# Slot weights by a difference and tanh, mask constants and half of the norm's rows on ScalarE, in the opening of a one-core transformer block

## What is computed

```python
mod = (silu(c) @ wmod).reshape(4, 6, 1, 128); sa, ca, ga, sb, cb, gb = ...
h = layernorm(x) * (1 + ca) + sa
q, k, v = h @ wq, h @ wk, h @ wv            # 16, 4, 4 heads of 64
logits = h @ wr                             # 16 heads, 4 nodes
tk_vals, tk_idx = top_k(logits, 2); tk_w = softmax(tk_vals)
member = one_hot(tk_idx, 4).sum(-2) > 0; pos = cumsum(member) - member
for n in range(4):                          # rotary at pos[..., n], causal, keys of node n only
    probs = softmax(where(causal & member[..., n], qr @ kr.T * 64**-0.5, -1e9)); outs[n] = probs @ v
y = (tk_w[..., None] * take(outs, tk_idx)).sum(3)
x = x + ga * (y @ wo)
x = x + gb * moe(layernorm(x) * (1 + cb) + sb)   # 8 routed choices, one is none, and a shared expert
```

## Time and profile before

| | us |
|---|---|
| median of 3 runs | 1045.87 |
| lowest and highest | 1040.52, 1046.56 |
| the profiled execution's own time | 1042.09 |
| its span | 1040.3 |
| TensorE busy | 880.0 (85%) |
| VectorE busy | 776.9 (75%) |
| ScalarE busy | 748.7 (72%) |
| GpSimd busy | 617.7 (59%) |

### The profile page before, as it was taken

The page is one execution under the profiler, slowest core; times in us unless marked ns, Lnnn a source line. Parts: engine busy times, 40 slices in busy tenths (PEclk is TensorE's granted clock), DMA queues, the critical chain, the costliest instruction groups (busy, mean ns, idle before and its releaser), DMA issues.

```text
span 1040.3 us, 18878 instructions
## 1 busy us (share of the span) xinstructions
PE 880.0 (85%) x5651; PEld 608.0 (58%) x5651; DVE 776.9 (75%) x1840; ACT 748.7 (72%) x2024; POOL 617.7 (59%) x869
## 2 busy tenths in 40 slices
PE   4338989999998998999899989999999996867883
PEld 3326656666666666656666657666676655534552
DVE  6999969957987797789778867996776755445443
ACT  6327787888888888877987888878887885333441
POOL 3157757857886786778677866886665630240222
PEclk9669989999999999999999999999999997789996
DMA  9000001001000000010000000010000041020003
GB/s 217 5 1 7 12 16 28 23 12 33 22 22 23 22 22 22 23 32 23 20 24 22 23 22 22 26 29 8 3 3 2 3 182 61 13 86 1 19 24 97
DMA packets 45602, 32.66 MB, mean 31 GB/s; under 512 B 8032, under 2 KB 43488, under 8 KB 45504
## 3 DMA queue, kind: packets, MB, share of 16 engines
q1 hardware_dynamic: 44288, 28.95, 9.7%
q0 software_dynamic: 1216, 2.51, 0.7%
HBM read 18.30 MB, written 12.36 MB: 29 GB/s over the span
## 4 chain that ended last, share of the span: by engine, by line
PE 63%; DVE 23%; ACT 6%; issue 5%; another core or an unknown queue 1%; POOL 1%; DMA 0%; ACTq 0%; DVEq 0%; POOLq 0%; SPq 0%
PE psum L1126 21%; PE psum L1148 7%; PE psum L1233 6%; PE psum L1140 6%; PE psum L1067 5%; PE psum L1111 4%; DVE pcs L805 3%; PE psum L1131 3%; DVE arena L753 3%; ACT probs L549 3%; DVE accs L861 2%; PE psum L1169 2%; DVE psum L850 2%; PE psum L1113 2%; PE psum L1128 2%
## 5 line engine op out<-in xcount | busy, mean ns | idle before, releaser
L1126 PE MATMUL psum<-QK 128*128 128x128 f32 (+3 forms) x1024 | 372.9, 449 | 4.9 <-ACT QK L528 4.9
L549 ACT ACTIVATE probs<-psum,negmax 128x128 f32<-128x128 f32 (+3 forms) x512 | 267.3, 530 | 108.3 <-DVE negmax L850 75.1
L390 POOL TENSOR_TENSOR R<-pcs 128x512 f32<-128x512 f32 x128 | 207.2, 1639 | 64.1 <-DVE pcs L805 46.8
L850 DVE CUSTOM_DVE_ANT_0 psum<-psum,causal 128x384 f32<-128x384 f32 (+1 forms) x256 | 156.9, 636 | 75.5 <-PE psum L1131 75.3
L1126 PEld LDWEIGHTS psum<-QK 128*128 128x128 f32 x1024 | 164.8, 193 | 49.3 <-issue 41.2
L416 POOL TENSOR_TENSOR coef<-rden,wslot 128x2 f32<-128x2 f32 x256 | 68.3, 267 | 177.2 <-DVE rden L856 177.1
L805 DVE TENSOR_TENSOR pcs<-psum,arena 128x512 f32<-128x512 f32 x256 | 161.6, 672 | 0.0
L861 DVE SCALAR_TENSOR_TENSOR accs<-probs,coef,accs 128x128 f32<-128x128 f32 (+3 forms) x256 | 157.6, 616 | 1.0 <-ACT accs L558 1.0
L558 ACT ACTIVATE accs<-probs,coef 128x128 f32<-128x128 f32 (+3 forms) x256 | 148.6, 581 | 11.5 <-POOL coef L416 10.7
L1140 PE MATMUL psum<-ident,accs 128*128 128x128 f32 x640 | 116.3, 280 | 46.5 <-ACT QK L528 41.9
L528 ACT ACTIVATE QK<-psum 128x384 f32<-128x384 f32 x256 | 126.7, 495 | 0.9 <-PE psum L1113 0.7
(11 more groups left out here) (211 smaller groups left out, 1473.3 us busy)
## 6 DMA issues: line engine op xcount, KB each, us to landing
weight_halves<-whl SPq DMA_DIRECT2D x48, 128.0 KB, 2.2
arena<-weight_halves SPq DMA_DIRECT2D x7, 768.0 KB, 7.1
wst<-in_L_ffn_w_up_dram SPq DMA_DIRECT2D x14, 128.0 KB, 2.6
wst<-in_L_ffn_w_gate_dram SPq DMA_DIRECT2D x14, 128.0 KB, 2.5
wst<-in_L_ffn_w_down_dram SPq DMA_DIRECT2D x14, 128.0 KB, 2.5
sorted_rows<-arena SPq DMA_DIRECT2D x1, 1430.0 KB, 12.1
QK<-sorted_rows SPq DMA_DIRECT2D x5, 260.0 KB, 4.0
x<-in_L_attn_x_dram SPq DMA_DIRECT2D x4, 256.0 KB, 4.1
```

The source lines that it names most:

```text
L390: pool.tensor_tensor(R[u][:, :, :, 0:3:2, half * HALF:(half + 1) * HALF].rearrange("p t e j f -> p (t e) j f"), halves(pc, half), halves(p ...
L549: act.activation((expB if e else expA)[:, k % (4 if e else 3), 0:w], area, ACT.Exp, scale=1.0 if k % TB < 2 else -1.0, bias=negmax[k % 4][ ...
L850: dve.tensor_tensor_reduce(score_area(k, e), score_area(k, e), causal[:, T - w:T], -1.0, 3e38, ALU.add, ALU.min, accum_out=negmax[k % 4][: ...
L1126: pe.matmul(o, QK[:, u, e, rows], QK[:, u, 2, 0:w], start=True, stop=False)
```

## The change

- The slot weights are no softmax over four logits but one difference: the logit of slot A less that of slot B, by `sA - sB` times the logits, summed (three VectorE operations after `first_angles(0)`); ScalarE makes tanh of half of it and from it both weights, 0.5 + 0.5 tanh and 0.5 - 0.5 tanh, between `trigonometry(0, 0)` and `trigonometry(0, 1)`. Five VectorE operations (L828 to L837) and one exponential are gone. The table preloaded there is now Silu's in place of Sin's.
- `cgap`, the reciprocal of the code difference (which is -1, -2 or -3), is made by a polynomial: two operations in place of `reciprocal`.
- Mask constants: a column `big_row`, 32768 at partition 32 and zero elsewhere, is made first on GpSimd; ScalarE writes the ring from it with scale 1 and -1, two activations for each buffer in place of one. The two GpSimd writes into partition 32 are gone.
- Norm, first turn only: ScalarE normalizes the last two of every four tiles (Identity with a scale and a bias column), VectorE the other two, after one more small operation for the bias.
- The scaling of the query weights (L478) moves behind the copies of the logits on ScalarE.

```diff
 @@ gpsimd
-            for t_, v in ((zero, 0.0), (ident, 0.0), ...
+            pool.memset(zero[:, :], 0.0).then_inc(S["const_done"], 1)
+            pool.wait_ge(S["const_done"], 1)
+            pool.affine_select(out=big_row[:, :], in_=zero[:, :], compare_op=ALU.not_equal, fill=BIG, base=-32,
+                               pattern=[[-1, 1]], channel_multiplier=1).then_inc(S["big_done"], 1)
+            for t_, v in ((one_half, 0.5), (ident, 0.0), ...
...
-            pool.wait_ge(S["zeros_done"], RING + 1)
+            pool.wait_ge(S["zeros_done"], 2 * RING + 1)
...
-            pool.wait_ge(S["ident_done"], 7)
-            pool.wait_ge(S["zero_set"], 2)
-            pool.memset(mring[32:33, :, 0, :], BIG).then_inc(S["mm_init"], 2)
-            pool.memset(mring[32:33, :, 1:3, :], -BIG).then_inc(S["mm_init"], 2)
-            pool.wait_ge(S["mm_init"], 4)
...
-            pool.wait_ge(S["w_done"], 1)
+            pool.wait_ge(S["w_done"], 2)
 @@ scalar
+            def mask_rows(r):
+                for kinds, sign in ((slice(0, 1), 1.0), (slice(1, 3), -1.0)):
+                    t_ = mring[:, r, kinds, :]
+                    act.activation(t_, big_row[:, :].unsqueeze(2).to_broadcast([P, t_.shape[1], T]), ACT.Copy, scale=sign
+                                   ).then_inc(S["zeros_done"], 1)
...
-            act.wait_ge(S["wr_in"], 32)
-            act.activation(w_qk[:, :, 0, :], w_qk[:, :, 0, :], ACT.Copy, scale=HD ** -0.5).then_inc(S["wq_scaled"], 1)
...
+                if turn == 0:
+                    act.wait_ge(S["rs_step"], 5)
+                    for t_ in range(NT):
+                        if t_ % TB >= 2:
+                            act.activation(xn[:, t_, :], x1[:, t_, :], ACT.Identity, bias=rs[:, 2, t_:t_ + 1],
+                                           scale=rs[:, 1, t_:t_ + 1]).then_inc(S["xn_a"], 1)
...
-            act.preload_act_table(ACT.Sin)
+            act.wait_ge(S["wr_in"], 32)
+            act.activation(w_qk[:, :, 0, :], w_qk[:, :, 0, :], ACT.Copy, scale=HD ** -0.5).then_inc(S["wq_scaled"], 1)
+            act.preload_act_table(ACT.Silu)
...
             trigonometry(0, 0)
+            act.wait_ge(S["w_step"], 3)
+            act.activation(lmax[:, 0, :], lmax[:, 0, :], ACT.Tanh, scale=0.5).then_inc(S["w_tanh"], 1)
+            act.wait_ge(S["w_tanh"], 1)
+            for e in range(2):
+                act.activation(wslot[:, :, e], lmax[:, 0, :], ACT.Identity, scale=0.5 - e, bias=one_half[:, 0:1]
+                               ).then_inc(S["w_done"], 1)
             trigonometry(0, 1)
             act.preload_act_table(ACT.Exp)
-            act.wait_ge(S["l_sub"], 1)
-            act.activation(ew[:, :], ew[:, :], ACT.Exp).then_inc(S["l_exp"], 1)
 @@ vector, normalize(turn)
+                if turn == 0:
+                    dve.scalar_tensor_tensor(rs[:, 2, :], mv[:, :, 0], -1.0, rs[:, 1, :], ALU.mult, ALU.mult
+                                             ).then_inc(S["rs_step"], 1)
                 for t_ in range(NT):
+                    if turn == 0 and t_ % TB >= 2:
+                        continue
 @@ vector, after first_angles(0)
-            dve.tensor_reduce(lmax[:, 0, :], L, AX_X, ALU.max).then_inc(S["l_max"], 1)
-            dve.wait_ge(S["l_max"], 1)
-            dve.tensor_tensor(W, L, lmax[:, 0, :].unsqueeze(2).to_broadcast([P, NS, NODES]), ALU.subtract
-                              ).then_inc(S["l_sub"], 1)
+            dif = prod[:, :, 0, :]
+            dve.tensor_tensor(dif, sA, sB, ALU.subtract).then_inc(S["w_step"], 1)
+            dve.wait_ge(S["w_step"], 1)
+            dve.tensor_tensor(dif, dif, L, ALU.mult).then_inc(S["w_step"], 1)
+            dve.wait_ge(S["w_step"], 2)
+            dve.tensor_reduce(lmax[:, 0, :], dif, AX_X, ALU.add).then_inc(S["w_step"], 1)
...
-            dve.reciprocal(cgap[:, :], lmax[:, 1, :]).then_inc(S["codes_done"], 1)
+            dve.scalar_tensor_tensor(cgap[:, :], lmax[:, 1, :], 6.0, lmax[:, 1, :], ALU.add, ALU.mult
+                                     ).then_inc(S["gap_done"], 1)
+            dve.wait_ge(S["gap_done"], 2)
+            dve.tensor_scalar(cgap[:, :], cgap[:, :], 11.0, -1.0 / 6.0, ALU.add, ALU.mult).then_inc(S["codes_done"], 1)
             first_angles(1)
             for e in range(2):
                 products(1, e)
-            dve.wait_ge(S["l_exp"], 1)
-            dve.tensor_tensor(prod[:, :, :, :], W.unsqueeze(2).to_broadcast([P, NS, 2, NODES]), sel[:, :, :, :],
-                              ALU.mult).then_inc(S["pr_w"], 1)
...
-            dve.tensor_reduce(es[:, :, :], prod[:, :, :, :], AX_X, ALU.add).then_inc(S["w_step"], 1)
...
-            dve.tensor_tensor(lmax[:, 1, :], es[:, :, 0], es[:, :, 1], ALU.add).then_inc(S["w_step"], 1)
...
-            dve.reciprocal(lmax[:, 0, :], lmax[:, 1, :]).then_inc(S["w_step"], 1)
...
-            dve.tensor_tensor(wslot[:, :, :], es[:, :, :], lmax[:, 0, :].unsqueeze(2).to_broadcast([P, NS, 2]),
-                              ALU.mult).then_inc(S["w_done"], 1)
 @@ tensor, norm_rows(turn)
-                    pe.wait_ge(S["xn_done"], turn * NT + (b + 1) * TB)
+                    if turn:
+                        pe.wait_ge(S["xn_done"], NT // 2 + (b + 1) * TB)
+                    else:
+                        pe.wait_ge(S["xn_done"], (b + 1) * TB // 2)
+                        pe.wait_ge(S["xn_a"], (b + 1) * TB // 2)
```

More of the change, by code:

```diff
@@ L63, in block_kernel @@
         zero = sb("zero", [P, 1])
+        one_half = sb("one_half", [P, 1])
+        big_row = sb("big_row", [P, 1])
         freq = sb("freq", [P, HALF])
@@ L196, in block_kernel @@
         names = """c_in wr_in loaded x_in0 x_in1 x_in2 x_in3 out_done const_done ident_done
[L197 to L200, removed]
+            mm_in0 mm_in1 mm_in2 c_exp c_sum c_rec c_silu mod_mm mod_raw mod_sign mod_mag mod_done
+            gcol_done ga_mm ga_ev wq_scaled bn_s bn_a var_e std_dev rs_step xn_done xn_a xn_t h_ready zeros_done big_done
+            lg_mm lg_ev rank_s rank_m w_tanh l_mem mem16 sel_a sel_b sel_cp code_p code_e gap_done
+            codes_done pos_mm pr_pos slots_w mk_t mk_ev w_step w_done
             ang_mul ang_k ang_n ang_r1 ang_r2 ang_clamp ang_abs trig_done qk_mm prod_done add_done q_done kd_done
@@ L295, in _ @@
             sp.wait_ge(S["mk_ev"], 6)
-            sp.wait_ge(S["mm_init"], 4)
+            sp.wait_ge(S["zeros_done"], 2 * RING + 1)
             for n in range(NH):
@@ L335, in _ @@
         def _(pool):
-            for t_, v in ((zero, 0.0), (ident, 0.0), (ident16, 0.0), (identbig, 0.0), (causal, 0.0), (before, 1.0),
+            pool.memset(zero[:, :], 0.0).then_inc(S["const_done"], 1)
+            pool.wait_ge(S["const_done"], 1)
+            pool.affine_select(out=big_row[:, :], in_=zero[:, :], compare_op=ALU.not_equal, fill=BIG, base=-32,
+                               pattern=[[-1, 1]], channel_multiplier=1).then_inc(S["big_done"], 1)
+            for t_, v in ((one_half, 0.5), (ident, 0.0), (ident16, 0.0), (identbig, 0.0), (causal, 0.0), (before, 1.0),
                           (ones16, 1.0), (ones, 1.0), (half_pi, float(np.pi / 2))):
@@ L340, in _ @@
                       allow_small_or_imprecise_dtypes=True).then_inc(S["const_done"], 1)
-            pool.wait_ge(S["const_done"], 10)
+            pool.wait_ge(S["const_done"], 11)
             for t_, v in ((ident, 1.0), (ident16, 1.0), (identbig, BIG)):
@@ L354, in _ @@
                       allow_small_or_imprecise_dtypes=True).then_inc(S["const_done"], 1)
[L355 to L356 removed]
+            pool.wait_ge(S["const_done"], 15)
+            pool.wait_ge(S["zeros_done"], 2 * RING + 1)
             pool.iota(zero_rows[:, :, DIM + 1].bitcast(U32), [[P, SORTED]], base=TOKENS, channel_multiplier=1
@@ L462, in _ @@
         def _(act):
[L463 to L467, removed]
+            def mask_rows(r):
[3 more added lines that the diff above has]
+                                   ).then_inc(S["zeros_done"], 1)
             act.wait_ge(S["const_done"], 1)
+            act.wait_ge(S["big_done"], 1)
             for r in range(2):
-                zeros(mring[:, r, :, :])
+                mask_rows(r)
             act.wait_ge(S["c_in"], 32)
@@ L474, in _ @@
             act.preload_act_table(ACT.Sqrt)
-            zeros(mring[:, 2, :, :])
-            zeros(zero_rows[:, :, :])
-            act.wait_ge(S["wr_in"], 32)
-            act.activation(w_qk[:, :, 0, :], w_qk[:, :, 0, :], ACT.Copy, scale=HD ** -0.5).then_inc(S["wq_scaled"], 1)
+            mask_rows(2)
+            act.activation(zero_rows[:, :, :], zero[:, :].unsqueeze(2).to_broadcast([P, SORTED, ROW]), ACT.Copy
+                           ).then_inc(S["zeros_done"], 1)
             def norm(turn, which, dst):
@@ L666, in normalize @@
                 dve.reciprocal(rs[:, 0, :], sd[:, :]).then_inc(S["rs_step"], 1)
-                dve.wait_ge(S["rs_step"], 4 * turn + 1)
+                dve.wait_ge(S["rs_step"], 5 * turn + 1)
```

(11 more changed lines are left out.)

7 lines of the change are left out of this document (removed).

## The result

The changed kernel takes 1036.89 us (median of 9 runs, 1035.15 to 1038.37) against 1046.56 of before (9 runs, 1040.33 to 1047.86). The ratio is 0.9928, 95% interval 0.9906 to 0.995. The profiled execution took 1035.15 us with a span of 1033.4, which is 6.9 less than before's span. The forecast was 1037.5, or -8.3 us from the median of before's first three runs. By the ratio the change is -7.5 us (-9.8 to -5.2); the quotient of the two medians, 0.9908, gives -9.7, since before's own times spread from 1040 to 1048.

A forecast was written before the change was run, and what follows sets the result against it. The opening was taken as a serial chain, mostly through VectorE, which stays the bound for a while behind it. Terms: -3.0 + 0.4 - 5.1 - 0.6 = -8.3 us, giving 1037.5 us as median; range 1030.5 to 1043, 8 in 10.

The forecast's parts named there:

- Modulation, -3.4: Opening, VectorE's small modulation operations: without GpSimd's mask writes, about 0.65 us in place of 4.07, so -3.4 us.
- Start, +0.25: Very start: ScalarE's split mask fills cost +0.25 us; GpSimd's new column is ready under ScalarE's first table load.
- Norm on two engines: Opening's norm: earlier tiles and transposes end the logits at 21.6 instead of 24.6 us; -3.0 including start and modulation.
- The logits' duration: Router logits on TensorE, behind the norm's transposes: taken to last 3.54 us, as in the old trace.
- second rival: Whole kernel, gain larger than forecast: -11.5 us, 1034 us; chance 0.20.
- Slot weights and loop start, +0.4 - 5.1: From slot weights to first row maximum: GpSimd's start comes 0.4 us later, the first row maximum 5.1 us earlier.
- Clock, -0.6: First scores: without TensorE's 4.93 us pause, early product pairs run at full clock; -0.6 of a possible 0 to -1.4 us.
- I carry the whole of it to the end: Attention loop: its steps depend only on each other, so the whole -8.3 us reaches the kernel's end.
- more than the sum: Attention loop: all 1.4 us of clock arrives and one later TensorE pause with slow restart vanishes; 1034 us, chance 0.20.
- The slower rival: First heads: TensorE's small waits grow to pauses costing 1.4 us each; with ten, 1051.5 us; chance 0.04.
- The ends of the sum, -10.4 and -6.5: Whole kernel: the total gain in us with all terms at their best and at their worst.
- The table loads: ScalarE around tanh and sine: a switch costs at most 1.3 us; two extra loads stay hidden or make the sum -7.3.

The follow-up runs named there:

- b_mask: Kernel before with only the mask constants changed (ScalarE writes the ring from a column, GpSimd's two writes gone); ratio to before 0.9989 (0.9966 to 1.0011).
- a_best2: Changed kernel plus 12 idle matmuls before the norm's transposes, 14 before the first scores, and ScalarE's table load first, second run; ratio to before 0.988.
- a_warm1: Changed kernel plus 12 idle TensorE matmuls ahead of the norm's transposes; ratio to before 0.9909 (0.9876 to 0.9942).
- a_norm_dve: Changed kernel with all 16 tiles of the norm on VectorE again; ratio to before 0.9943 (0.9919 to 0.9966).
- b_weights: Kernel before with only the slot weights changed (difference, tanh, polynomial for the gap); ratio to before 0.9964 (0.9935 to 0.9992).
- a_again2: Changed kernel, unedited, profiled once more on another chip; one run, 1024.48 us.
- b_again: Kernel before, unedited, run again as a kernel of its own; ratio to before 1.0006 (0.9983 to 1.0028).
- b_warm1: Kernel before plus 12 idle TensorE matmuls ahead of the norm's transposes; ratio to before 0.999 (0.9968 to 1.0012).
- a_sin: Changed kernel with the table preloaded for Sin in place of Silu; one run, 1024.40 us.
- a_again: Changed kernel, unedited, run again on another chip; ratio to before 0.9931 (0.9899 to 0.9963).

## Why the prediction was right

*Modulation, -3.4.* Right. The operations take 0.70 us (11.90 to 12.60) where they took 4.16 (11.04 to 15.20), and they do so with GpSimd's writes gone and nothing else changed in the norm (b_mask).

*Start, +0.25.* Mis-sized: 0.86 (11.04 to 11.90). The step that failed is that "GpSimd's new column is ready under ScalarE's first table load". The load itself came behind the wait for the column, at 1.40 us and not 0.81; put ahead of it, it gives 0.6 back (a_best2). The rest is the split fills, as forecast.

*Norm on two engines.* The durations were right (a tile every 0.39 us; ScalarE's copies late next, seen as 0.70 us in a_warm1). But the split gives nothing, since the transposes bound the stage from 14.7 on either way: they start and end alike in a_norm_dve. Whether it would give something behind the idle matmuls was not tried. "3.70 us whatever feeds them" is itself a duration at the low clock: behind the idle matmuls they take 2.94 (a_warm1). A slip of the sum: 17.95 + 3.54 is 21.5, not 21.6. With fast logits the whole stands at 22.7 to 23.4 instead of 22.2 for the start of the ranks, -1.9 to -2.6 against -3.0.

*The logits' duration.* The step that fails is the unsaid one in "then the logits start, which took 3.54 us": a duration read from one trace at 2.4 GHz was taken as the code's. It is 4.3 or 7.1 in traces of one program, and 3.7 in others with the same logits code. In after's trace this term alone turned some -2.5 into +0.85. That the profiled span still came out near the forecast is luck: the loop gave 3.6 us that the forecast had left out (its second rival hadn't). The ratio over nine executions, where such draws mix, is nearer to a test of the sum, with 2.3 us either way.

*Slot weights and loop start, +0.4 - 5.1.* Right in sum: -5.1 in b_weights, and -4.4 to -5.2 in all kernels with the part and without the second group of idle matmuls, by how much of the first scores is slow: the stretch at 0.50 ends between 71 and 72 us in a_again2 and between 74 and 75 in after. The +0.4 was +0.25 in after (from the ranks to the second angles 30.40 us, before 30.15), since the gap's first operation was cheaper than its row (0.42 us and not 0.6). One reason given is not the one: ScalarE's exponential didn't keep it from QK. The copy that ended TensorE's pause of 4.93 us stood in ScalarE's list behind L549, which had waited 6.43 us for the late first row maximum.

*Clock, -0.6.* Right in kind, somewhat smaller. The pause of 4.93 us and its fall are gone from all ten traces with the new weights and present in before, b_again, b_mask and b_warm1 (from 76 to 80 us on). From the first row maximum to that of the second head it takes 10.41 to 10.68 us in these four and 9.98 or 9.99 in eight of the ten, so -0.4 to -0.7. In a_warm1 it takes 10.16, and in after, whose first scores were slow longest, 10.44: there the term gave nothing.

*"I carry the whole of it to the end".* Not in one execution. The loop's length follows the count of falls: 694.6 to 694.9 us with one, 695.9 to 696.5 with two, 697.2 to 698.4 with three, 699.1 and 699.6 with four, so about 1.5 us each, near the 1.4 that the prediction gave a slow restart. After's trace had two falls fewer than before's: by this price 3 of the 3.6 us that its loop was shorter, which hid that the logits had lost as much. Whether the gain arrives whole on average is not shown: the ratio allows 5.2 to 9.8 us. The rival "more than the sum" had this mechanism; it came together with a start that was smaller than forecast. The slower rival needed six falls more; no trace had more than four. The ends of the sum, -10.4 and -6.5, are wider than the bounds given for its terms, which add up to -10.0 and -7.0.

*The table loads.* The trace agrees with the 1283 ns of the Trainium skill (ScalarE: Activation LUTs, What ACT_TABLE_LOAD costs): 1.28 us in a_sin. The drain of 1380 ns that it adds doesn't show: in the earlier trace rows the exponential starts 0.01 us behind its load. With Silu's table preloaded, sine, tanh and sine ran without a load between them (after); with Sin's, tanh and the second sine had one each (a_sin), which cost nothing here.

Open: what decides whether a pause of TensorE ends in a fall. A fall between 139 and 149 us comes in 11 of the 14 traces, one between 204 and 216 in 6, in kernels with and without the change, and nothing tried here says beforehand in which. With the idle matmuls ahead of the transposes the logits took 3.76 us in three of three traces of the changed kernel; without them the length is a draw. That the new weights lower their number is not shown beyond the one at 79.

## What to carry to other kernels

Before a duration on TensorE goes into a sum, compare it with the same shape elsewhere: 421 ns against 275 for one matmul, or 7.06 us against 3.68 for the group, was the clock level here, and it may be the other one next time. A gain in an opening ahead of a loop with pauses arrives only give or take a fall or two; take several traces before explaining the last 3 us. ScalarE's first table load belongs ahead of its first wait (0.6 us here), and long GpSimd writes do not belong beside VectorE's small operations if those are on the critical path (3.4 us here).

## What the runs showed of the hardware

- The column of the granted clock reads 1.00 from the start of each trace to the first fall. In after it does so from 0 to 47 us, while the logits' matmuls (18.4 to 25.0) and the projection of values (29.1 to 30.6) take 421 ns each. In before the same projection takes 421 where the column reads 0.50 and 275 where it reads 1.00. Durations tell the level there, the column doesn't.
- In after TensorE was busy from 16 to 26 us without a break (2.00 of 2.00 us in each window of 2 us), and still all the logits' matmuls up to 25.0 took 421 to 445 ns.
- GpSimd's write into one partition, 1536 elements, takes 1.37 us, and VectorE's operations on 4 elements (in each partition) last as long: 1.40 us against 0.24 for the same two without it (b_mask). By what way the one holds the other is not shown.
- Behind the last copy of values the same program takes 264.7 us in after and 253.5 and 253.6 in a_again and a_again2, on another chip; before's takes 264.5 and 266.2 (b_again).
